# Two passes of masked attention written out by hand: another order of the instructions of four queues

## What is computed

```python
q = x @ Wq.T + bq;  k = key @ Wk.T + bk;  v = value @ Wv.T + bv      # N = 4096 rows, D = 512
s = (q @ k.T) / sqrt(4096) * adj                                     # 4096 x 4096
s = where(abs(s) < 1e-5, -1e9, s)
x1 = layernorm(x + (softmax(s) @ v) @ Wm.T + bm)
out = layernorm(x1 + relu((adj @ x1) @ W.T + b))
```

## Time and profile before

| | us |
|---|---|
| median of 3 runs | 2370.11 |
| lowest and highest | 2366.82, 2374.42 |
| the profiled execution's own time | 2356.89 |
| its span | 2355.1 |
| TensorE busy | 2010.8 (85%) |
| VectorE busy | 1550.6 (66%) |
| ScalarE busy | 865.7 (37%) |
| mean granted TensorE clock | 0.939 of 2.4 GHz |

### The profile page before, as it was taken

How to read it: one execution, slowest core, us unless ns; L and a number is a source line. 1 busy time by engine, 2 the same in 40 slices (tenths; PEclk the granted TensorE clock), 3 DMA queues, 4 the chain that set the end, 5 groups by cost and what they waited for, 6 DMA issues and landing times.

```text
span 2355.1 us, 26353 instructions
## 1 busy us (share of the span) xinstructions
PE 2010.8 (85%) x8859; PEld 890.7 (38%) x8859; DVE 1550.6 (66%) x3203; ACT 865.7 (37%) x1166; POOL 107.0 (5%) x158
## 2 busy tenths in 40 slices
PE   8958888889888888798888888888886690999998
PEld 5423333333333333333333333333332240444443
DVE  7976666677777755466666666666665240787877
ACT  6764434544554444344444444444443100000000
POOL 5000000000000020000000000000000000000000
PEclk9989998999999999899999999999998795999999
DMA  8467766788788796866666666666665949654542
GB/s 302 178 173 170 190 185 161 195 219 221 188 226 204 191 232 180 165 154 150 150 153 153 152 150 155 151 152 153 154 152 179 241 75 73 154 141 116 146 111 80
DMA packets 585959, 393.21 MB, mean 167 GB/s; under 512 B 479729, under 2 KB 506353, under 8 KB 584049
## 3 DMA queue, kind: packets, MB, share of 16 engines
q1 hardware_dynamic: 565088, 306.26, 53.7%
q0 software_dynamic: 20752, 85.47, 14.6%
HBM read 190.32 MB, written 117.44 MB: 131 GB/s over the span
## 4 chain that ended last, share of the span: by engine, by line
PE 39%; DVE 20%; SPq 13%; issue 10%; DMA 10%; ACT 8%; DVEq 0%; ACTq 0%
PE ps L1144 14%; PE ps L988 8%; PE ps L1009 7%; DMA PT<-Phl 6%; PE ps L1020 4%; DVE Phl L1906 3%; DVE prob L1878 3%; SPq L457 3%; SPq L461 3%; SPq L584 3%; PE ps L1105 2%; PE ps L1033 2%; ACT small L1348 2%; DMA UT<-Uhl 2%; DVE prob L1890 2%
## 5 line engine op out<-in xcount | busy, mean ns | idle before, releaser
L988 PE MATMUL ps<-KG,left 128*128 128x512 f16 x2688 | 662.7, 397 | 144.2 <-ACT ps L1341 127.4
L1009 PE MATMUL ps<-V,PT 128*128 128x512 f16 x3072 | 710.3, 382 | 7.4 <-issue 7.4
L988 PEld LDWEIGHTS ps<-KG,left 128*128 128x128 f16 x2688 | 268.2, 101 | 503.4 <-issue 207.6
L1009 PEld LDWEIGHTS ps<-V,PT 128*128 128x128 f16 x3072 | 302.8, 99 | 377.8 <-issue 21.7
L1348 ACT ACTIVATE small<-prob 128x512 f32<-128x512 f32 x256 | 160.8, 628 | 548.3 <-DVE prob L1878 547.8
L1906 DVE SCALAR_TENSOR_TENSOR Phl<-prob,Phl 128x2048 f16<-128x2048 f32 x64 | 146.3, 2286 | 139.8 <-DMA PT<-Phl 134.6
L1884 DVE TENSOR_SCALAR small<-small,eps_s,neg_s 128x512 f32<-128x512 f32 x256 | 139.6, 545 | 119.4 <-ACT small L1348 107.2
L1020 PE MATMUL ps<-Wvm,UT 128*128 128x512 f16 x384 | 112.8, 456 | 84.6 <-issue 57.3
L1890 DVE CUSTOM_DVE_ANT_0 prob<-prob,small 128x512 f32<-128x512 f32 x256 | 175.6, 686 | 2.6
L1341 ACT ACTIVATE ps<-ps 128x512 f32<-128x512 f32 x192 | 111.6, 581 | 153.0 <-PE ps L988 153.0
L1566 ACT ACTIVATE p<-ps 128x512 f32<-128x512 f32 x14 | 8.4, 597 | 395.3 <-PE ps L1144 395.3
(11 more groups left out here) (222 smaller groups left out, 2018.3 us busy)
## 6 DMA issues: line engine op xcount, KB each, us to landing
adjh<-in_adj POOLq DMA_DIRECT2D x64, 512.0 KB, 5.6
adj_bf<-adjh SPq DMA_DIRECT2D x64, 512.0 KB, 4.3
left_dram<-left SPq DMA_DIRECT2D x16, 896.0 KB, 4.3
xraw<-in_x_t SPq DMA_DIRECT2D x8, 1024.0 KB, 8.8
t_dram<-tq POOLq DMA_DIRECT2D x8, 1024.0 KB, 5.9
t<-t_dram SPq DMA_DIRECT2D x32, 256.0 KB, 3.3
x_in<-in_x SPq DMA_DIRECT2D x32, 256.0 KB, 3.6
xb_dram<-x_in SPq DMA_DIRECT2D x32, 256.0 KB, 2.7
```

The lines of the kernel that those rows point to most:

```text
L988: last = nc.tensor.matmul(ps[:, bank, :], left[:, s, k, d * P:(d + 1) * P], KG[gr][:, RIGHT[k], m, d, :], start=(first and n == 0), stop=( ...
L1009: last = nc.tensor.matmul(ps[:, BU + b, :], PT[:, b, s, m, :], V[:, v, m, :], start=(m == 0 and n == 0), stop=(m == MT - 1 and n == 2))
```

## The change

The instructions stay the same but for their order and place. On TensorE `weigh` of a tile begins one part later, and `project` and `rows_product` move to other places, with other semaphores to wait on. ScalarE exponentiates the tiles of period `q` at the beginning of period `q + 1`, VectorE makes the last maximum there, and both engines' other steps are rearranged. The SP queue's order follows, and pairs of transfers that stood together are split. Period 0 of the first pass is written out apart. The diff, cut to parts of SP, TensorE (the passes, then the tail), ScalarE and VectorE:

```diff
+                    turn_high(2 * q - 1)
+                    turn_low(2 * q - 1)
                     if q >= 2:
-                        store_first(before - 1)
+                        store_first(2 * q - 3)
                     if q + 1 < NP:
-                        for b in range(2):
-                            load_x_first(2 * (q + 1) + b)
+                        if q == 1:
+                            store_x_bias(4)
+                            load_x_first(6)
+                        store_x_bias(2 * (q + 1) + 1)
                     if 2 <= q < 6:
                         load_chunk(2 * (q - 2))
+                    if q + 2 < NP:
+                        load_x_first(2 * (q + 2) + 1)
+                    if FIRST_STEP <= q < FIRST_STEP + STEPS:
+                        store_second_values(q - FIRST_STEP)
...
+                    if i >= 2:
+                        turn_merged_high(2 * i - 4)
+                        turn_merged_low(2 * i - 4)
+                    turn_high(2 * q - 2)
+                    turn_low(2 * q - 2)
...
                     scores(q, 0, P1)
                     scores(q, 0, P7)
                     if q >= 2:
-                        weigh(g1 - 2, 2)
+                        weigh(g1 - 2, 1)
+                    if i >= 3:
+                        rows_product(2 * i - 5)
                     scores(q, 0, P6)
                     scores(q, 0, P2)
                     if q >= 2:
-                        weigh(g1 - 2, 3)
+                        weigh(g1 - 2, 2)
+                    if i >= 2:
+                        project(2 * i - 4)
                     scores(q, 0, P5)
                     scores(q, 0, P4)
                     if q >= 2:
+                        weigh(g1 - 2, 3)
+                    scores(q, 0, P3)
+                    if q >= 1:
                         weigh(g0, 0)
-                    scores(q, 0, P3)
-                    if q == 1:
-                        weigh(g0, 0)
+                    if q == 6:
+                        scale_turn(S_K2, BX)
+                    scores(q, 1, P1)
+                    scores(q, 1, P7)
                     if q >= 1:
                         weigh(g0, 1)
                     if i >= 2:
-                        project(2 * i - 3, s_z, 2 * i - 3)
-                    if q == 6:
-                        scale_turn(S_K2, BX)
-                    if q == NP:
-                        scale_turn(S_1, BX)
-                    scores(q, 1, P1)
-                    scores(q, 1, P7)
+                        rows_product(2 * i - 4)
+                    scores(q, 1, P6)
+                    scores(q, 1, P2)
                     if q >= 1:
                         weigh(g0, 2)
                     if i >= 2:
-                        rows_product(2 * i - 4, s_z, 2 * i - 2)
-                    scores(q, 1, P6)
-                    scores(q, 1, P2)
-                    if q >= 1:
-                        weigh(g0, 3)
+                        project(2 * i - 3)
                     scores(q, 1, P5)
                     scores(q, 1, P4)
                     if q >= 1:
-                        weigh(g1, 0)
-                    if i >= 2:
-                        rows_product(2 * i - 3, y_cp, 2 * i - 3)
+                        weigh(g0, 3)
                     if q == 6:
                         scale_turn(S_V2, BX)
                     scores(q, 1, P3)
                     if q >= 1:
-                        weigh(g1, 1)
-                    if i >= 1:
-                        project(2 * i - 2, y_cp, 2 * i - 2)
+                        weigh(g1, 0)
+                    if q == NP:
+                        scale_turn(S_1, BX)
...
-                last_unit = 2 * NT - 1
-                for part in (2, 3):
-                    weigh(last_unit - 2, part)
-                rows_product(NT - 4, s_z, NT - 3)
-                for part in range(MC):
-                    weigh(last_unit - 1, part)
-                project(NT - 3, y_cp, NT - 3)
-                for part in range(MC):
-                    weigh(last_unit, part)
-                rows_product(NT - 3, s_z, NT - 2)
+                last = 2 * NT - 1
+                weigh(last - 2, 1)
+                rows_product(NT - 5)
+                weigh(last - 2, 2)
+                project(NT - 4)
+                weigh(last - 2, 3)
+                weigh(last - 1, 0)
+                weigh(last - 1, 1)
+                rows_product(NT - 4)
+                weigh(last - 1, 2)
+                project(NT - 3)
+                weigh(last - 1, 3)
+                weigh(last, 0)
+                weigh(last, 1)
+                rows_product(NT - 3)
+                weigh(last, 2)
+                project(NT - 2)
+                weigh(last, 3)
 
                 pe.wait_ge(s_adj, OUT * group(2 * NP, 0))
-                aggregate(0, 0, 0, 8)
-                project(NT - 2, y_cp, NT - 2)
-                aggregate(0, 0, 8, NP)
-                project(NT - 1, s_z, NT - 1)
+                aggregate(0, 0, 0, NP)
+                rows_product(NT - 2)
+                project(NT - 1)
                 aggregate(0, 0, NP, NT - TC)
                 aggregate(0, 1, 0, 8)
-                rows_product(NT - 2, s_z, NT)
+                rows_product(NT - 1)
                 aggregate(0, 1, 8, NT - TC)
                 pe.wait_ge(u_mg, NT)
                 aggregate(1, 0, 0, 8)
...
                 def first_period(q):
+                    exponentials(q - 1, 0)
                     seed(q, 0, AB)
-                    if q >= 1:
-                        prob_high(q - 1, 1)
+                    prob_high(q - 1, 0)
+                    exponentials(q - 1, 1)
                     seed(q, 0, EP)
-                    if q == 0:
-                        key_high(1, P1)
                     seed(q, 0, BCU)
+                    if FIRST_STEP <= q < FIRST_STEP + STEPS:
+                        second_keys_high(q - FIRST_STEP)
                     seed(q, 0, BU2)
-                    if q == 0:
-                        key_high(1, P7)
-                        key_high(1, P6)
-                    else:
-                        magnitude(q, 0, C11)
+                    seed(q, 0, CD)
+                    prob_high(q - 1, 1)
+                    magnitude(q, 0, C11)
+                    if FIRST_STEP <= q < FIRST_STEP + STEPS:
+                        second_values_high(q - FIRST_STEP)
+                    magnitude(q, 0, C22)
+                    seed(q, 1, AB)
                     if q >= 2:
-                        copy_first(2 * (q - 2) + 1)
-                    seed(q, 0, CD)
-                    if q == 0:
-                        key_high(1, P2)
-                        magnitude(q, 0, C11)
-                        key_high(1, P5)
-                    magnitude(q, 0, C22)
+                        copy_first(2 * q - 3)
+                    seed(q, 1, EP)
                     magnitude(q, 0, C21)
-                    if q == 0:
-                        key_high(1, P4)
-                        key_high(1, P3)
-                    if FIRST_STEP <= q < FIRST_STEP + STEPS:
-                        second_highs(q - FIRST_STEP)
                     magnitude(q, 0, C12)
-                    seed(q, 1, AB)
-                    seed(q, 1, EP)
                     seed(q, 1, BCU)
                     seed(q, 1, BU2)
-                    magnitude(q, 1, C11)
                     if q + 1 < NP:
                         t_high(q + 1, False)
+                    magnitude(q, 1, C11)
                     seed(q, 1, CD)
                     magnitude(q, 1, C22)
                     magnitude(q, 1, C21)
-                    if q >= 1:
-                        copy_first(2 * (q - 1))
-                    exponentials(q, 0)
-                    magnitude(q, 1, C12)
-                    prob_high(q, 0)
                     if q + 1 < NP:
                         t_high(q + 1, True)
-                    exponentials(q, 1)
-
-                for q in range(NP):
+                    magnitude(q, 1, C12)
+                    copy_first(2 * q - 2)
+
...
                 def first_period(q):
-                    if q >= 1:
-                        prob_low(q - 1, 0)
-                        if q == 6:
-                            scale_square(S_K2, mcol[:, 2 * MC:3 * MC], kv_mx, 4 * MC)
-                        if FIRST_STEP <= q < FIRST_STEP + STEPS:
-                            second_sums(q - FIRST_STEP)
-                        prob_low(q - 1, 1)
-                    masked(q, 0, C11)
-                    if q == 0:
-                        key_low(1, P1)
-                        key_low(1, P7)
-                    small_scores(q, 0, C11)
-                    added(q, 0, C22)
-                    threshold(q, 0, C11)
-                    masked(q, 0, C22)
-                    if q == 0:
-                        key_low(1, P6)
-                        key_low(1, P2)
-                    added(q, 0, C21)
-                    small_scores(q, 0, C22)
```

(44 more changed lines are left out.)

493 lines of the change are left out of this document (290 added, 203 removed).

## The result

| | kernel before | changed kernel |
|---|---|---|
| median, us | 2372.3 (2366.8 to 2384.8, 4 runs) | **2227.6** (2225.5 to 2249.5, 4 runs) |
| profiled execution: time, span | 2356.9, 2355.1 | 2225.5, 2223.7 |
| TensorE busy in the span | 2010.8 (85%) | 1986.5 (89%) |

What follows compares the result with a forecast made beforehand. TensorE was taken to set the pace in both passes, with some 7 to 9 us of waiting per period. Terms summing to -240 took 2356.9 to 2117, plus 13 for the median: 2130 us, range 2083 to 2192.

Steps and rivals of the forecast that it cites:

- Second pass: Fourteen periods from 18 on: waits go and a period falls from 58.5 to 50.0 us, -119 (ends -129 and -84).
- `project`, CD and `merge`: Second pass: waits of 4.33 us before `project` and 1.12 for copy CD go; `merge` ahead of C21 costs nothing.
- Two signs: Second pass: no wait ahead of `project`; wrong if VectorE's low halves wait for `PT` over 5 us in mid-pass.
- First pass, periods 7 to 14: TensorE's waits for ScalarE mostly go; a period falls from 46.7 to 40.5 us, lower bound 38.9: -50 us.
- the later part: First pass: weighing begins at 16.8 us of a period, some 3.9 later, leaving about 2 us of slack.
- Periods 2 to 5: First pass, with chunk loads: VectorE's wait for the chunk stays; 50.1 us per period becomes 46.3, -15.
- 5.9 + 1.5: Periods 2 to 5: 5.9 us per period of kept chunk wait, plus 1.5 for slow matmuls behind the gap.
- Periods 15 to 17: Around the change of passes: period 15 saves 3 us, `left` costs +2, periods 16 and 17 save 8.
- The collision: At the end: `Tb` leads the `adj` transposes by 5.7 us; TensorE's wait falls from 57.81 to 15, -43.
- The Trainium skill's rule on arbitration: At the end: engines go round queues packet by packet, making the wait now 0; the forecast held the trace contradicts it.
- Rival 4: Both passes: slow low-half transposes close the loop from exponential to `PT` to weighing; slower, 2460 us; chance 0.03.
- Rival 3: First pass bound by transfers: transposes land 5 us later, a period stays at 44; 2186 us; chance 0.12.

Runs made afterwards that it cites:

- e6: Changed kernel with `store_adj` back behind the first pair of `PT`'s transposes in the second pass from period 18 on; 2095.3 us in one run.
- e1: Changed kernel, but from period 18 on GpSimd's two `adj` loads also wait until both transposes of tile 2q-2 have landed; 2102.5 us.
- e8: Changed kernel with `weigh` back in its earlier slots in the first pass alone; 2240.7 us in one run.
- e10: Kernel before with `weigh` one slot later in the first pass; 2373.1 us in one run, beside 2371.5.
- e2: Kernel before with the last `rows_product` moved ahead of the 56 matmuls of `aggregate` in front of it; 2300.8 us.
- e4: Changed kernel, but the loads of `Tb` wait for `f_mm` = 2, to leave with the transposes of `adj`; 2216.9 us in one run.
- e12: e11 with SP's two loads of `zf` moved directly ahead of the transposes of `adj`; 2284.5 us in one run.
- e11: e4 with three memsets on GpSimd ahead of the `Tb` loads, which start some 1.5 us later; 2240.4 us in one run.

## Why the prediction was wrong, point by point

- **Second pass, forecast -119, measured +7.4.** This step failed, and with it the number. Its working prices `project`, CD and `merge`, and nowhere the move of `store_adj` to the end of SP's period, though GpSimd's next load waits for that store. I had the price in hand: the same crawl in the earlier trace rows. With the move undone (e6) or its effect gated (e1), the fourteen periods take 702.5 and 703.9 us; I had written 50.0 x 14 = 700. So the rest of the step was right, `merge` included. Two signs that I had named failed: `project` had waits of up to 12.9 us where I had forecast none, and the wait for `PT` was there, though I had looked for it at VectorE's low halves. It stood at ScalarE's high halves, for 141.8 us (50.0 before), and VectorE waited behind them:

```profile
POOL adjh L821 <- DMA adj_bf<-adjh: 806.4, 28, 60.5
...
ACT Phl L1398 <- DMA PT<-Phl: 141.8, 19, 17.9
```

  The first row is the new wait: 28 loads wait for the store, where VectorE's masks released 62 of the 64 before.
- **First pass, periods 7 to 14, forecast 40.5 us each, measured 38.9.** The size was right within 2 us, at the lower bound, and the reason was not, so the number came near by luck: I said that the later part buys the time, and e8 and e10 show that it buys none. I added 1.6 us per period for transfers at a DMA share near 1; at 1.01 they still cost nothing.
- **Periods 2 to 5, forecast a wait kept, 46.3 us each.** Right in kind: four waits of 3.2 to 4.1 us stand there, and the periods take 43.9 us, counted as the forecast counted them (50.1 before). The price of 5.9 + 1.5 was too high by 10 us in all.
- **Periods 15 to 17, forecast -9, measured -1.1.** The two waits that I had left as they were have grown: 10.10 us for `left` (8.99 before), and in period 17, where the values are loaded beside the transposes, 15.69 and 5.38 us for ScalarE, where 1.48, 7.47 and 4.47 stood before.
- **The collision, forecast a wait of 15, measured 0.** The order of events was right (`Tb` 6.4 us ahead of the transposes, 5.7 forecast), and e2 shows that order to be worth 58.6. But the head start of `Tb` was not needed: in e4 `Tb` leaves behind the transposes and TensorE does not wait either. I took the crawl for what any overlap of the two queues does; e4 and e12 show that it also needs SP's plain loads just ahead, and the same move took them away (from 1924.92, directly ahead of the transposes at 1926.79, to 1843.76, 9.1 us ahead of those at 1852.86). My reason had no such step, and the term came near by luck.
- **The Trainium skill's rule on arbitration.** I let the trace of before speak against it. The counts of e4 agree with it (204 to 204), those of e12 do not (241 to 65). The page has some 9 to 17 descriptors in a packet, and no run here shows whether the profile counts such packets or single descriptors, so the rule is not settled either way. And neither count tells why a packet of the transposes holds an engine so much longer in the crawl.
- **The rivals.** None had the right place. Rival 4 had the mechanism, a slow transpose closing the loop, but tied it to 4 MB of values. Rival 3 fell: at a share of 1.01 no transfer held the first pass up. The changed second pass repeats: 822 to 843 us for its fourteen periods in five runs with the same code there (e4, e8, e11, e12 and the changed kernel itself), so the miss is no accident of one run.

## What to carry to other kernels

When a store on one queue is moved, list who waits for its landing on the other queues, and look at what those will then start beside. Do not give a DMA transpose both unfinished plain transfers of its own queue ahead of it and a load of GpSimd's queue that starts with it; in these runs one of them put a few us earlier or later removed the harm at no cost that showed. And test an explanation on its own even where the forecast number came true: the slot that gives a change its name may do nothing.

## What the runs showed of the hardware

- The two transposes of a pair of row blocks of `adj` are issued in 10.5 us with nothing large beside them (one such pair of the changed kernel, at 1877.03), in 21.5 us beside 4 MB from GpSimd's queue (e11), and in 67.5 us (e12) if two plain loads of 256 KB precede it by 1 us (78.6 in the kernel before). In e12 its queue's packets hold the engines for 100.9% of the time at 0.06 MB in 5 us.
- In the good case (e4), two queues side by side move 395 GB/s, with as many packets of one as of the other, and the transposes are only put off. A packet of the transposes holds an engine for about 0.02 us then, and for 0.19 (changed kernel) to 0.33 us (e12) in the crawl; these are estimates from the packet counts and shares of the DMA views.
- TensorE ran 38.9 us without a gap, at full clock, at a DMA share of 1.01 and 250 GB/s: full DMA queues alone did it no harm there.
